# Expert blocks of 256 slots instead of 128, and a gate in front of the first scatter and the last gather

## What is computed

```python
xn = _layernorm(x)
x = x + _L0_attn_ref(xn, ...) + _L0_ffn_ref(xn, ...)     # RWKV-like recurrence; 16 small experts
xn = _layernorm(x)
x = x + _L1_attn_ref(xn, ...) + _L1_ffn_ref(xn, ...)     # 16 heads causal; 8 experts, two rounds
```

```python
for _ in range(2):
    z_norm = _rmsnorm(z, norm_w)
    topk_vals, topk_idx = top_k(softmax(z_norm @ router_w), 2)
    for e in range(8):
        mixed = mixed + cw[:, e:e+1] * ((silu(z_norm @ w1[e]) * (z_norm @ w3[e])) @ w2[e])
    z = z + mixed
```

## Time and profile before

| | |
|---|---|
| median of three runs | 1879.63 us (1879.26 to 1882.79) |
| the profiled execution | 1881.2 us, its span 1879.9 us |
| first layer and normalisation | 0 to about 740 us |
| second layer, before the first block of experts | to 883.1 us |
| first to last block (156) | 883.1 to 1786.1 us |
| rest of the attention, last gather, output | to 1879.9 us |
| TensorE busy, of the span | 81% |
| VectorE, ScalarE, GpSimd busy | 63%, 48%, 20% |
| DMA | 177 MB, 94 GB/s on average |

### The profile page before, as it was taken

One profiled execution on the slowest core, in us unless ns is written; L12 is line 12 of the kernel. 1 busy time (PEld: TensorE's weight loads), 2 busy tenths in 40 slices (PEclk: granted clock), 3 DMA queues, 4 the chain that ended last, 5 costly groups with the idle time before them and its releaser, 6 DMA issues.

```text
span 1879.9 us, 28828 instructions
## 1 busy us (share of the span) xinstructions
PE 1531.4 (81%) x10452; PEld 717.1 (38%) x10452; DVE 1184.1 (63%) x3013; ACT 902.9 (48%) x1375; POOL 380.8 (20%) x351
## 2 busy tenths in 40 slices
PE   5679898988989898526888898889887898888946
PEld 1233233323323322213443444454444544444512
DVE  4674677668567734867564667766667666666612
ACT  1246666656656666301444454535444355435534
POOL 4001121211211112060320003205142051410050
PEclk8769898988999898555898899969998899899977
DMA  6112122212222221212443344424443254533310
GB/s 209 31 56 70 65 89 77 73 64 86 71 71 87 76 80 63 71 45 61 128 139 87 111 122 130 118 84 137 123 127 106 79 154 135 141 112 109 107 50 23
DMA packets 139005, 177.06 MB, mean 94 GB/s; under 512 B 18768, under 2 KB 93136, under 8 KB 138608
## 3 DMA queue, kind: packets, MB, share of 16 engines
q1 hardware_dynamic: 130528, 158.02, 27.8%
q0 software_dynamic: 8192, 16.79, 3.1%
q10 hardware_dynamic: 144, 0.40, 0.1%
HBM read 133.34 MB, written 41.81 MB: 93 GB/s over the span
## 4 chain that ended last, share of the span: by engine, by line
PE 60%; DVE 19%; ACT 9%; issue 6%; another core or an unknown queue 3%; DMA 2%; SPq 1%; POOL 0%; DVEq 0%; ACTq 0%
PE ax_sums L1759 7%; PE m_up L469 5%; PE sh_bank L2250 5%; PE m_sums L486 5%; PE wide L1781 4%; PE wide L1672 4%; PE sh_bank L2261 4%; DVE wide L1703 3%; PE sh_bank L2281 3%; ACT m_act_h L509 3%; PE m_sums L497 3%; DVE am_top L1708 2%; PE rw_bank L711 2%; ACT ax_prob L1813 1%
## 5 line engine op out<-in xcount | busy, mean ns | idle before, releaser
L1813 ACT ACTIVATE ax_prob<-wide 128x1024 f32<-128x1024 f32 (+1 forms) x320 | 298.8, 939 | 313.8 <-PE wide L1789 102.7
L509 ACT ACTIVATE m_act_h<-m_up,const 128x1024 f32<-128x1024 f32 x256 | 278.4, 1113 | 204.7 <-PE m_up L469 204.2
L1703 DVE CUSTOM_DVE_ANT_0 wide<-wide,const 128x384 f32<-128x384 f32 (+3 forms) x512 | 238.4, 517 | 119.7 <-PE wide L1672 101.3
L2186 POOL DMA_INDIRECT x<-slot_results,mr_slots x128 | 122.1, 954 | 496.6 <-PE wide L1781 184.3
L1708 DVE TENSOR_REDUCE am_top<-wide 128x2 f32<-128x1024 f32 x128 | 156.1, 1222 | 102.0 <-PE wide L1672 96.0
L1672 PE MATMUL wide<-al_ks,al_qs 48*128 48x512 bf16 (+3 forms) x768 | 129.8, 366 | 85.4 <-DVE am_top L1708 27.5
L1759 PE MATMUL ax_sums<-ax_prob,al_vs 128*32 128x512 f32 (+3 forms) x1536 | 179.3, 539 | 23.5 <-ACT ax_prob L1813 23.5
L2169 POOL DMA_INDIRECT slot_tokens<-mr_zn,mr_slots x128 | 124.2, 971 | 348.1 <-PE wide L1789 136.4
L555 POOL TENSOR_TENSOR m_prod<-m_prod 128x512 f32<-128x512 f32 x64 | 89.2, 1397 | 517.8 <-DVE m_prod L525 517.8
L469 PE MATMUL m_up<-m_terms,w1s 96*128 96x512 bf16 x512 | 161.0, 413 | 13.0 <-ACT m_act_h L509 13.0
L486 PE MATMUL m_sums<-m_act_h,const 128*32 128x512 f32 x1024 | 148.2, 654 | 25.9 <-DVE m_prod L525 20.5
(11 more groups left out here) (299 smaller groups left out, 2248.8 us busy)
## 6 DMA issues: line engine op xcount, KB each, us to landing
m_wt<-in_experts SPq DMA_DIRECT2D x156, 384.0 KB
m_share<-shares SPq DMA_DIRECT2D x128, 256.0 KB
m_rows<-slot_tokens SPq DMA_DIRECT2D x156, 64.0 KB
slot_results<-m_y SPq DMA_DIRECT2D x156, 64.0 KB
stack<-mp_part SPq DMA_DIRECT2D x48, 128.0 KB
m_terms<-stack SPq DMA_DIRECT2D x64, 96.0 KB, 2.0
qstack<-ap_qpart SPq DMA_DIRECT2D x48, 128.0 KB
al_qs<-qstack SPq DMA_DIRECT2D x32, 192.0 KB
```

Source lines behind the costliest of these rows:

```text
L509: A.activation(self.act_h[:, slot, :, :], self.up[u][:, :, :], ACT.Gelu, bias=self.w("b1", 4 * half + ep, 4 * half + ep + 1)).then_inc(sel ...
L1703: p = V.tensor_tensor_reduce(tile[:, x, first:first + n], tile[:, x, first:first + n], self.w("later_s", TILE - n, TILE), -1.0, 3e38, ALU. ...
L1813: A.activation(dst, src, ACT.Exp, scale=SCALE).then_inc(*wide.empties("sum", i, u))
```

## The change

- `BLOCK` is 256, `NBLK` = 16 + 7 = 23, 92 blocks in all; the blocks' pitch is 8.1 places. Each load, copy, matmul by w1 and w3 and product takes 256 slots; the transpose becomes two, the matmul by w2 four.
- The first scatter and the last gather wait for `wide` tiles too; their pitch `GATHER` is 1.6 and not 1.25, and the blocks begin at place 100 and not 93.
- The last additions stand later: the last phase's by `LATE`, its last one behind the last projection of the attention's output.
- Six of the eight projection chunks stand earlier.
- To make room, `key` and `values` lie in `x`, and the squares of the router's norm in its `turned`; for that ScalarE waits for the product of the phase before, and VectorE for the projections' stores at task 2 instead of 4.

```diff
-        self.key = sb("k", TILE)
+        self.key = x[:, 0:TILE]
-        self.values = [sb(f"values{n}", NC, VW) for n in range(2)]
+        self.values = [x[:, TILE + n * NC * VW:TILE + (n + 1) * NC * VW].rearrange("p (n v) -> p n v", v=VW) for n in range(2)]
...
-BLOCK = 128
+BLOCK = 256
-GATHER = 1.25
+GATHER = 1.6
-STEP = 4.78
+STEP = 8.1
-BLOCKS = [93.0 + (STEP * NBLK + 3.0) * ph for ph in range(len(PHASES))]
+BLOCKS = [100.0 + (STEP * NBLK + 3.0) * ph for ph in range(len(PHASES))]
+SCATTER[1] = max(SCATTER[1], SCATTER[0] + SCATTERS[0] * 2 * GT)
+LATE = 1.36
-PROJECT_AT = [11.7, 18.4] + [slot_at(x) for x in (1.6, 2.1, 2.9, 3.4, 3.9, 4.4)]
+PROJECT_AT = [11.7, 18.4] + [slot_at(x) for x in (1.4, 1.85, 2.3, 2.75, 3.2, 3.65)]
...
-            uses["t", ph, b], uses["a", ph, b], uses["b", ph, b], uses["y", ph, b] = at - 1.2, at, at + 1.1, at + STEP + 0.55
+            uses["t", ph, b], uses["a", ph, b], uses["b", ph, b], uses["y", ph, b] = at - 1.6, at, at + 1.5, at + STEP + 0.75
...
-                if i == NG and th == 0:
+                if i == 2 and th == 0:
                     for c in range(NT):
                         start.all_sent(v, c)
...
-        self.sq = [sb(f"sq{n}", NC, HID) for n in range(2)]
+        self.sq = [self.turned[:, n * NC:(n + 1) * NC, :] for n in range(2)]
+                a.wait_ge(*shared.full("logits", ph - 1))
...
-        self.rows = [sb(f"rows{n}", HID) for n in range(3)]
+        self.rows = [sb(f"rows{n}", 2, HID) for n in range(3)]
-        self.y = [sb(f"y{n}", HID) for n in range(2)]
+        self.y = [sb(f"y{n}", 2, HID) for n in range(2)]
...
-                    if ph:
-                        g_.wait_ge(wide.filled, wide.in_front(here))
+                    g_.wait_ge(wide.filled, wide.in_front(here))
...
-                        if ph + 1 < len(PHASES):
-                            g_.wait_ge(wide.filled, wide.in_front(here))
+                        g_.wait_ge(wide.filled, wide.in_front(here))
...
-        E.transpose(shared.bank("t", ph, b)[:, 0:BLOCK], self.rows[n % 3][:, :], self.w("ident")).then_inc(shared.filled, 1)
+        for s in range(2):
+            p = E.transpose(shared.bank("t", ph, b)[:, s * CH:(s + 1) * CH], self.rows[n % 3][:, s, :], self.w("ident"))
+        p.then_inc(shared.filled, 1)
...
-        for f in range(2):
-            p = E.matmul(shared.bank("y", ph, b)[:, 0:HID], self.hid[n % 2][:, f * BLOCK:(f + 1) * BLOCK],
-                         self.wt[n % 4][:, 2 * MF + f * HID:2 * MF + (f + 1) * HID], start=f == 0, stop=f == 1)
+        for s in range(2):
+            if s:
+                yield shared.within("y", ph, b)
+            for f in range(2):
+                p = E.matmul(shared.bank("y", ph, b)[:, s * HID:(s + 1) * HID], self.hid[n % 2][:, f * BLOCK + s * CH:f * BLOCK + (s + 1) * CH],
+                             self.wt[n % 4][:, 2 * MF + f * HID:2 * MF + (f + 1) * HID], start=f == 0, stop=f == 1)
...
+    def combined_at(self, ph, c):
+        last = ph + 1 == len(PHASES)
+        at = COMBINE[ph] + GATHERS[ph] * (LATE if last else 1.0) * 2 * NC * (c + 1) + 2.5
+        return max(at, self.shared.place["out_p", NT - 1] + 1.0) if last and c + 1 == GC else at
```

20 lines of the change are left out of this document (10 added, 10 removed).

## The result

Four runs of the changed kernel have a median of 1823.54 us (1821.34 to 1824.37) beside 1880.25 us (1879.26 to 1882.79) for the kernel before: ratio 0.9695, 95% interval 0.9678 to 0.9711. Forecast were 1845 us, 1815 to 1878. The gain, 57 us, is 22 us more than forecast.

The account below looks back on a forecast made before the run. The prediction took TensorE's own work to pace the middle and late semaphores to hold up both ends. Opening +5, middle -16 and closing -24 sum to -35 us, from a median of 1879.63 to 1845 us, range 1815 to 1878.

Parts of the forecast that it names:

- Opening, forecast +5: Up to the first block: 18 us for its later place, 16 taken back from late semaphores, 3 of standing.
- The standing at the first block: Opening: TensorE would stand 3 us because the last gated scatter comes late; ends 0 and 5.
- the later place: Opening: 7 more attention tiles and a projection chunk before the first block would cost 18 us.
- Closing, forecast -24: After the last block: -22 from gated gathers, -4 for three tiles fewer, +2 for the late additions.
- The gate: Closing: gathers waiting for attention tiles would take back 22 of 33.8 us of late semaphores; ends 0 and 33.8.
- rival A: Closing isn't cleared: GpSimd still issues each 1.25 us and semaphores stay late; 22 us lost, 1867 us, chance 0.20.
- Middle, forecast -16: Between first and last block: +39 for more columns, -48 for 280 fewer rows, -3 for tiles, -4 for a projection chunk.
- Edits costed at nothing: ScalarE and VectorE copies, block row loads, weight traffic and waits from overlaid buffers: all valued at 0 us.
- The wait for a block's rows: TensorE waiting for a block's loaded rows, read as 9 times, 8.3 us; change valued 0, ends -8 and +10.
- B: Middle: 18% more columns are paid and saved changes of subject give nothing back; middle +32, 1893 us, chance 0.10.
- C: Middle: passes of 256 columns cost the same 0.11 us as passes of 128; 1761 us, chance 0.03.
- D: Both ends: late semaphores don't come from GpSimd's pace, so both stand as long as before; 1883 us, chance 0.07.

Follow-up runs that it names:

- a_nogate: The changed kernel with the first scatter and last gather again not waiting for attention tiles: 1845.76 us, ratio 0.9799 to the kernel before.
- b_nosplit: The kernel before with the halves of w1, and of w3, side by side on TensorE, 114 rows fewer: 1837.61 us, ratio 0.9996.
- b_smallweights: The kernel before with only 128 of 768 columns of an expert's weights loaded from the fifth block on: 1835.36 us, ratio 0.9999.
- b_gates: The kernel before with only the two waits for attention tiles added, at the old pitch of 1.25: 1848.77 us, ratio 0.9827.
- after_again: The changed kernel, unaltered, run again beside the kernel before on a third chip: 1810.43 us, ratio 0.9854.
- a_pitch_again: The changed kernel with pitch 1.25 and blocks from place 93, on the third chip: 1797.35 us, ratio 0.9778 to the kernel before.
- b_ends_proj: The kernel before with all of the change except blocks of 256 and overlaid buffers, so with early projections: 1869.55 us, ratio 0.9926.
- a_halfcols: The changed kernel with w1 and w3 multiplying only 128 of a block's 256 slots from the fifth block on: 1793.41 us, ratio 0.9493.
- b_ends: The kernel before with gates, pitch 1.6, blocks from place 100 and late additions, but 128-slot blocks and projections unmoved: 1826.22 us, ratio 0.9940.
- a_nosplit: The changed kernel with the halves of w1, and of w3, side by side on TensorE, 67 rows fewer: 1814.29 us, ratio 0.9885.

## Why the late semaphores went, and where they never were

Four profiles have a train of indirect DMAs 1.25 us apart and no gate at both ends. Before and a_nogate show the pieces of 5 to 20 us, b_nosplit and b_smallweights show none. The train is the same in b_nosplit as in the earlier trace rows:

```profile
1776.49 0.94 POOL L2186 DMA_INDIRECT x<-slot_results,mr_slots  x1 [134.11 <-issue]
1777.74 0.94 POOL L2186 DMA_INDIRECT x<-slot_results,mr_slots  x1 [0.31 <-issue]
```

and yet TensorE, ScalarE and VectorE go on. Neither these two nor any of the other six profiles of the second and third chips has the unknown queue in its chain by engine. In seven of the eight the chain could be followed back only to some point between 810 and 820 us, inside the opening, so its shares add up to about half of the span; the list of waits of all engines, from 740 us to the end, has none on an unknown queue in any of the eight either. For b_nosplit the chain reads:

```profile
PE 33%; DVE 12%; issue 5%; ACT 2%; DMA 1%; POOL 1%; SPq 1%; ACTq 0%; DVEq 0%
```

So two things are needed: the train, which a gate breaks (a_nogate and b_gates, on one chip), and a chip, or a state of one, on which it hurts. It costs the kernel before 18.4 us in the opening (98.8 - 80.4) and 22.6 in the closing (94.1 - 71.5), 41 of the 46 us between the chips. The chain had charged 33.8 us to the closing, 11 more than their absence gives. The likely reason is a wait that is there without them, VectorE's for the gathered rows (b_nosplit, closing):

```profile
DVE zt L2353 <- DMA x<-slot_results,mr_slots: 27.3, 4, 12.2
```

Behind it TensorE's sums stand for VectorE's copy (line 1828), 11.7 us in the same stretch. In the closing of after_again the row reads:

```profile
DVE zt L2370 <- DMA x<-slot_results,mr_slots: 0.5, 1, 0.5
```

The late additions alone don't take that wait away. a_pitch_again has them too, at the old pitch and with the blocks from place 93, and there it reads:

```profile
DVE zt L2370 <- DMA x<-slot_results,mr_slots: 19.4, 2, 13.5
```

What is gone in both is most of the standing behind it: TensorE's sums wait 2.7 us for VectorE's copy in a_pitch_again, and no such wait is left in after_again.

What in a chip makes the semaphores late is open. That the result's pair and the four experiments of the first chip show pieces on the unknown queue (in b_ends_proj and a_halfcols of at most 5 us, in the closing) and the other eight don't is all I have; it could be the chip, its neighbours' work, or where the program lay.

## The prediction, point by point

**Start.** The attention's first tile comes 1.4 us earlier in the profile after, nothing of the change.

**Opening, forecast +5, measured -5.3 from the first tile.** The pieces give back 18.4 of 18.8 us (16 forecast). The standing at the first block came as costed, 3.5 us for 3. The term that was mis-sized is the later place: it costs 9.6 us (80.4 to 93.5, less the 3.5) and I had 18. It was 24 more matmuls on the attention's tiles (97 to 121), not 17, with the projection chunk, and they went by at 0.40 us each and not at the 0.83 that I took from the average of the opening. b_ends reaches its first block after 93.4 us too and doesn't stand there, so what sets that time, the tiles or the gated scatter, isn't separated.

**Closing, forecast -24, measured -21.2. The sum is right by luck, the terms are not.** The gate was to give 22 us. By itself it gave 14.0 in the kernel before (b_gates) and 9.9 in the changed one (a_nogate). Against the chips without late semaphores, 22.6 us are late before and 14.5 after (72.9 - 58.4), so 8.1 count in this sum. This is rival A in good part, with the reason that I gave for it: with the gate open GpSimd goes at its 1.25 us again. The step that failed under it was to take the chain's 33.8 us as the price, where 22.6 is what their absence gives.

The rest, -13.1 us (71.5 to 58.4 where no semaphore is late), is what I had put at -4 for three tiles and +2 for the late additions. b_ends has it too (55.6), so it belongs to the ends and not to the blocks. a_pitch_again splits it, roughly, since its blocks have 256 slots and those of b_nosplit 128. With the late additions, but the old pitch and place, the closing takes 66.7 us: 4.8 less than 71.5, although 141 matmuls of attention tiles are left behind the last block there and not 135. The pitch and the places, which leave 122, bring the other 8.3 us, 0.44 us for each of 19 matmuls. So the edit that I charged 2 us for paid, since the attention's work stands less behind VectorE, and the tiles paid more than I had.

**Middle, forecast -16, measured -32.0.** By the prediction's own account, passes at full clock were 494 us (223, 226 and 45) and are 523 (36 more, and 3 and 4 less). I divided both by 0.92 and got +32. The stretch now runs at 0.95: 494 / 0.92 = 537 and 523 / 0.95 = 551, +14. That is the term that was mis-sized, by some 18 us (the clock is read to two digits, 3 us either way): the clock was taken as given. What is left, 366 and 320 us, falls by 46 for 280 rows: 0.16 us each, and I had taken 0.17.

The number held, by luck; its reading as a price of a row did not. b_nosplit and a_nosplit save rows at 0.08 to 0.11 us of busy time and give all of it back. What blocks of 256 do besides is to cut the chains through the three banks from 156 to 92. Groups by line on TensorE, from the first to the last block, before (busy us, mean ns, idle before them and what ended it):

```profile
L2250 PE MATMUL sh_bank<-m_tok,m_wt 128*128 128x128 f32 x620 | 130.3, 322 | 29.1 <-issue 16.8 <-ACT m_tok L2309 5.0 <-DVE m_hid L2345 4.4
L2261 PE MATMUL sh_bank<-m_tok,m_wt 128*128 128x128 f32 x620 | 124.3, 310 | 23.3 <-DVE m_act L2338 12.2 <-DVE ao_scaled L1878 4.7 <-DVE mr_base L2096 2.9
L1672 PE MATMUL wide<-al_ks,al_qs 48*128 48x512 bf16 (+3 forms) x674 | 108.6, 347 | 29.9 <-DVE am_top L1708 10.6 <-DVE am_later L1703 8.4 <-DVE am_top L1703 5.5
```

and after:

```profile
L2252 PE MATMUL sh_bank<-m_tok,m_wt 128*128 128x256 f32 x364 | 121.4, 443 | 8.9 <-issue 6.4 <-ACT m_tok L2316 1.6 <-DVE ao_scaled L1881 0.6
L2263 PE MATMUL sh_bank<-m_tok,m_wt 128*128 128x256 f32 x364 | 105.6, 400 | 5.7 <-DVE m_act L2345 5.7
L1675 PE MATMUL wide<-al_ks,al_qs 48*128 48x512 bf16 (+3 forms) x660 | 104.5, 340 | 69.1 <-DVE am_top L1711 26.8 <-DVE am_later L1706 17.0 <-DVE am_top L1706 15.6
```

Standing before the products by w1 and w3 falls from 52.4 to 14.6 us; standing before the attention's "max" tiles rises from 29.9 to 69.1, most of it on VectorE's row maxima. All standing together hardly moves (120.5 and 117.8 us), and the gain lies in busy time. Why saved rows are kept here and not in the two experiments I can argue, fewer chains need less cover, but no run shows it by itself. The fair pair, b_ends and after_again, puts the blocks at 15 us with the rows, the early projections and the clock (0.92 and 0.94) in it. The other 13 us of the middle, before to b_ends (902.7 to 889.6, on two chips), go with the four tiles and the projection chunk, which I had at 7; no run splits them.

**Edits costed at nothing.** ScalarE's 596 ns and VectorE's 684 are as read; VectorE's wait for the tanh is 46.1 us for the 35.6 of the earlier trace rows, with little work behind it that TensorE waits for (5.7 us at line 2263). The wait for a block's rows was misread and mis-sized. The earlier trace rows counts weight loads (5.4 us) together with matmuls (2.9 us in 3 times), and by the same view it has tripled:

```profile
  DMA m_rows<-slot_tokens: 25.7, 27
```

At the matmuls alone it is 9.5 us in 9 times, 3.5 of them at the first block: 6.6 more than before, where I had put 0; by the view of the earlier trace rows it is 17.4 more, beyond the end of 10 that I gave it. How much of it is on the path isn't shown. Not foreseen either: with blocks of 128 the early projections go with 27 us more in the first phase (267.6 and 240.7, on two chips, the longer from an execution 8 us over its median). With blocks of 256 that phase takes 238.4 us; no run has them with the projections at their old places.

**Rivals.** A came in part: 14.0 us stay on an unknown queue where it had 22. B fell: the middle is 871, not 935, though a_nosplit shows its mechanism alive for some rows. C fell by the passes' 0.21 us. The Trainium skill ("TensorE: Matmul & The Clock Gate", section on the back-to-back issue gap) gives a sustained spacing of about 81 ns at 128 columns and 131 ns at 512, by which 256 columns would cost far less than twice 128. These f32 passes cost in proportion, 0.11, 0.21 and 0.43 us at 128, 256 and 512 columns. But a_halfcols shows that a pass removed is worth some 0.4 of its duration in this middle (30 of 75 us), so with C's premise the time would still not have been 1761. D fell on the first chip, where the gates alone gave 33 us. The Trainium skill ("SBUF — State Buffer", section on who interferes with whom) has TensorE and ScalarE never wait for GpSimd; the second and third chips agree. The section speaks of ports, and what held the updates back on the result's chip for 18.4 and 22.6 us isn't shown.

**The signs that were named.** No unknown queue in the opening: so. Under 12 us in the closing: 14.0, no. First block near 888: 876.4. A middle of 887: 870.7, between that and the 850 that was to speak for C or a dearer row. 70 us after it: 72.9. A long wait at the first block, for a late scatter: 3.5 us. Middle and closing are inside their bounds and 1823.5 is inside the range, but the opening's -5.3 is outside its own ends, -0.8 to +13.

## What to carry to other kernels

Before charging a long piece of the chain to a cause, look at what the same engines wait for under it: a row of "idle before" on a consumer's line (here 20.0 us of VectorE for gathered rows) can point to a second prize, here 5 us or more for a changed place in the order. Compare a row of waits with the same view of it. Put waits on a far DMA behind the work that others wait for, and gate a train of indirect DMAs by progress elsewhere; in the opening the gate costs nothing (80.4 us with it on the first chip and without it on the second), and at both ends together it gave 33 us where semaphores were late. At the closing it cleared only part, because a gate that stands open is none. Moving the same matmuls side by side only turned busy time into standing; merging blocks, which removes whole chains between engines, kept its gain (15 us in the fair pair).

## What the hardware showed that I had not expected

- The same kernel took 1880 us on one chip and 1835 to 1838 on two others, each over 13 to 23 runs. Some 41 of the 46 us go with updates of semaphores that come 5 to 20 us late while GpSimd issues indirect DMAs 1.25 us apart, and they appear on the slow one alone. A ratio from one chip (0.9695) doesn't hold on another (0.9854).
- The granted clock isn't fixed when work is added or taken out: with 75 us of passes left out the middle's clock went from 0.95 to 0.90 and busy time fell by 38 us only; with the change it went from 0.92 to 0.95, at the same busy share (86.7% and 86.5%), which by the sum above gave some 18 us.
- An indirect DMA of 128 rows lands about 1.54 us behind its issue of 0.96: a train in which each waits for the one before runs at 2.5 us each, twice the 1.25 us of the free train.
